# Hybrid layer on one core: norm statistics inside the mixer loop, the token table and all gate-up products ahead of the down products

## The reference, cut to what matters

```python
x = x + mixer(layernorm(x), ...)                    # state-space mixer, 8 groups of 1024 channels
x = x + ffn(layernorm(x), ...)                      # FFN, run 0
x = x + layernorm(x) @ (weight * block_mask).T      # block-sparse projection 512 -> 512
x = x + ffn(layernorm(x), ...)                      # FFN, run 1, same weights

def layernorm(x):  return (x - mean(x)) / sqrt(var(x) + 1e-5)

def ffn(x):
    g, u = split(x @ shared_w_gate_up.T, 2)         # 512 wide each
    shared = (silu(g) * u) @ shared_w_down.T
    probs = softmax(x @ gate_w.T)                   # 16 experts
    v, idx = top_k(probs, 2);  v = v / sum(v)
    # expert e: silu(x @ Wg_e.T) * (x @ Wu_e.T), 128 wide, then @ Wd_e.T
    moe = sum over the token's two experts of v * expert(x)
    return moe + shared
```

## Time and profile before

| what | value |
| --- | --- |
| median of 3 runs | 2115.55 us (2114.65 to 2116.76) |
| the profiled execution's own time | 2115.74 us |
| its span | 2114.0 us |
| granted TensorE clock, mean | 0.982 of full speed |
| busy share of the span | PE 94%, weight loads 78%, DVE 67%, ACT 55%, POOL 50% |
| mixer loop ends, all engines meet | 1666.1 us |
| first gate-up product, run 0 and run 1 | 1686.47 and 1920.41 us |

### The profile page before, as it was taken

One profiled execution on the slowest core, in us unless ns is written; L12 is line 12 of the kernel. 1 busy time (PEld: TensorE's weight loads), 2 busy tenths in 40 slices (PEclk: granted clock), 3 DMA queues, 4 the chain that ended last, 5 costly groups with the idle time before them and its releaser, 6 DMA issues.

```text
span 2114.0 us, 39207 instructions
## 1 busy us (share of the span) xinstructions
PE 1984.8 (94%) x11776; PEld 1643.1 (78%) x11776; DVE 1422.0 (67%) x2710; ACT 1172.9 (55%) x2553; POOL 1067.3 (50%) x955
## 2 busy tenths in 40 slices
PE   3899999999999999999999999999999889988998
PEld 2688878788878888888878888878888678766776
DVE  6697589749875976697579748974986551286214
ACT  2596368537843874496469537853884225321441
POOL 1288149705951793189239814970695125320423
PEclk8899999999999999999999999999999999999999
DMA  2453035114512341343135204521450349813895
GB/s 84 133 155 87 25 116 163 58 45 123 160 50 71 109 138 41 87 133 102 36 96 160 81 26 119 168 63 37 122 156 25 108 150 399 314 51 115 297 386 164
DMA packets 143908, 261.75 MB, mean 124 GB/s; under 512 B 19536, under 2 KB 35920, under 8 KB 143696
## 3 DMA queue, kind: packets, MB, share of 16 engines
q1 hardware_dynamic: 134848, 231.35, 34.6%
q0 software_dynamic: 7520, 24.65, 3.6%
q10 hardware_dynamic: 1328, 3.15, 0.4%
HBM read 233.38 MB, written 25.69 MB: 123 GB/s over the span
## 4 chain that ended last, share of the span: by engine, by line
PE 31%; issue 28%; DVE 23%; POOL 14%; ACT 2%; DVEq 1%; POOLq 0%; DMA 0%; ACTq 0%; SPq 0%
PE bank L1492 19%; DVE Y L1203 7%; POOL Y L711 7%; PE bank L1775 5%; DVE Y L1212 3%; PE bank L1787 3%; DVE mem L1171 3%; DVE mem L1191 3%; DVE Y L1228 2%; POOL wl L694 2%; POOL Y L661 1%; POOL spare L687 1%; POOL cv L687 1%; PE bank L1762 1%; POOL mem L673 1%
## 5 line engine op out<-in xcount | busy, mean ns | idle before, releaser
L1492 PE MATMUL bank<-xh,wh 128*128 128x512 f32 x1288 | 524.3, 407 | 16.5 <-POOL wl L694 12.9
L1492 PE MATMUL bank<-xh,wl 128*128 128x512 f32 x1288 | 505.5, 392 | 0.0
L1492 PE MATMUL bank<-xl,wh 128*128 128x512 f32 x1288 | 503.0, 391 | 0.0
L694 POOL TENSOR_TENSOR wl<-raw,wh 128x512 fp32r<-128x512 f32 x144 | 184.0, 1283 | 487.2 <-ACT wh L846 487.2
L1203 DVE SCALAR_TENSOR_TENSOR Y<-bank,cpar,Y 128x511 f32<-128x511 f32 (+2 forms) x384 | 287.0, 747 | 22.8 <-ACT Y L891 13.8
L1492 PEld LDWEIGHTS bank<-xh,wh 128*128 128x128 f32 x1288 | 243.4, 189 | 65.0 <-issue 18.0
L1492 PEld LDWEIGHTS bank<-xh,wl 128*128 128x128 f32 x1288 | 242.6, 188 | 54.4
L1492 PEld LDWEIGHTS bank<-xl,wh 128*128 128x128 f32 x1288 | 243.9, 189 | 46.0 <-issue 0.5
L1492 PE MATMUL bank<-wh,ah 128*128 128x512 f32 x576 | 229.4, 398 | 17.8 <-DVE al L1419 17.2
L1492 PE MATMUL bank<-wl,ah 128*128 128x512 f32 x576 | 227.0, 394 | 0.0
L1492 PE MATMUL bank<-wh,al 128*128 128x512 f32 x576 | 226.9, 394 | 0.0
(11 more groups left out here) (214 smaller groups left out, 3880.0 us busy)
## 6 DMA issues: line engine op xcount, KB each, us to landing
mem<-c_rows SPq DMA_DIRECT2D x128, 256.0 KB, 3.8
mem<-wffn_d SPq DMA_DIRECT2D x62, 512.0 KB, 8.2
E<-e_rows SPq DMA_DIRECT2D x256, 96.0 KB, 3.4
raw<-wconv_d SPq DMA_DIRECT2D x80, 256.0 KB, 2.8
cv<-c_rows SPq DMA_DIRECT2D x64, 256.0 KB, 3.9
spare<-c_rows SPq DMA_DIRECT2D x64, 256.0 KB, 4.2
raw<-wgate_d SPq DMA_DIRECT2D x64, 256.0 KB, 2.7
raw<-wout_d SPq DMA_DIRECT2D x64, 256.0 KB, 2.6
```

Of the source, the lines that this page charges most:

```text
L694: inc(pool.tensor_tensor(wl[:, W_SLOT[p], :], raw[:, R_SLOT[p], :], wh[:, W_SLOT[p], :], ALU.subtract), w_lo)
L1492: got = mm(out, l, r, start=first and n == 0, stop=last and n == 2)
```

## The change

Four things move. (1) In the mixer loop DVE takes the statistics of tile t - 1 behind the sum of tile t, in every group (only those of the last group are used), and the means of tiles 0 to 3 behind the sum of tile 6. ACT computes their square root and splits two weight pieces of the first shared block before the engines meet, for which SP loads four pieces before they meet. SP then asks for the mask ahead of the sparse weight. (2) `FFN_ORDER` has all four gate-up pairs ahead of all down products, in all four shared blocks; the hidden values of j = 2, 3 get places of their own in free rows of `wh` and `wl` (`hidden_rows`). (3) DVE computes the token table from the slots by a bit mask in place of five wide instructions, and between the parts of `hidden`; PE's `tokens` stands ahead of the down products. `own` moves behind the token list. (4) In the second blocks combine and sums are put in another order on DVE, and all six weight pieces for the third shared block are split inside norm 2.

```diff
@@ mixer loop, vector engine
                     t = k - NORM_AT
                     if 0 <= t < TT:
+                        if t:
+                            now(dve, res_ok, i, t)
+                        if t == CH + 2:
+                            now(dve, x_st, i, CH)
                         now(dve, big_mm, i, NCONV + NGATE + t + 1)
                         inc(STT(X[:, t, :], bank[big_bank(NCONV + NGATE + t)][:, :], rs8[:, t:t + 1], X[:, t, :],
                                 ALU.mult, ALU.add), res_ok)
+                        if t:
+                            inc(nc.vector.bn_stats(bst[:, t - 1, :], X[:, t - 1, :]), x_st)
+                        if t == CH + 2:
+                            for s in range(CH):
+                                inc(nc.vector.bn_aggr(mv[:, s, :], bst[:, s, :]), x_mv)
@@ vector engine, behind the loop
+            inverse1(0)
             phase_end(dve, PH_MIXER)
-            layer_norm(1)
+            xn1(0)
+            xn1(1)
+            stats1(TT - 1)
+            means1(1)
+            xn1(2)
+            lo1(0)
...
@@ scalar engine
-            phase_end(act, PH_MIXER)
+            deviations(1, 0)
...
+            for p in range(2):
+                w_part(0, p)
+            phase_end(act, PH_MIXER)
             layer_norm(1)
-            for p in range(6):
+            for p in range(2, 6):
                 w_part(0, p)
@@ order of the shared blocks, places of the hidden values
-        FFN_ORDER = [("gu", 0, 0), ("gu", 1, 0), ("gu", 0, 1), ("dn", None, 0), ("gu", 1, 1), ("dn", None, 1)]
+        FFN_ORDER = [("gu", 0, 0), ("gu", 1, 0), ("gu", 0, 1), ("gu", 1, 1), ("dn", None, 0), ("dn", None, 1)]
+        def hidden_rows(i, j, low):
+            if j < 2:
+                return (al if low else ah)[:, j, :, :]
+            s = (10, 0)[j - 2] if i % 2 else 7 + j
+            return (wl if low else wh)[:, s, :].rearrange("p (a b) -> p a b", a=4)
@@ vector engine, first shared block
-                hidden(first, 0)
-                hidden(first, 1)
+                hidden_gate(first, 0)
+                hidden_up(first, 0)
                 places()
-                for t in range(CH):
-                    add_down(first, t)
+                hidden_lo(first, 0)
+                hidden_gate(first, 1)
+                hidden_up(first, 1)
+                tiles_of_slots()
+                hidden_lo(first, 1)
+                rows_of_slots()
                 hidden(first, 2)
-                tokens_of_slots()
+                toks_out()
+                owners()
                 hidden(first, 3)
-                toks_out()
-                for t in range(CH, TT):
+                for t in range(TT):
                     add_down(first, t)
@@ vector engine, second shared block
+                hidden(second, 2)
                 combine(2)
-                hidden(second, 2)
                 combine(3)
-                for t in range(CH):
-                    dve.wait_ge(cmb, 2 * TT * run + 2 * (t + 1))
-                    add_down(second, t)
+                hidden(second, 3)
                 combine(4)
-                combine(5)
...
+                for t in range(CH):
+                    combined_down(t)
+                    if t == 1:
+                        combine(5)
+                    if run == 0:
                         stats2(t)
...
-                hidden(second, 3)
                 combine(6)
@@ tensor engine, first shared block
-                    if n == 4:
+                    if n == 3:
                         tokens()
```

More of the change, by code:

```diff
@@ L562, in _ @@
                 first, second = 2 * run, 2 * run + 1
+                for p in range(NRAW):
+                    shared_in(first, p)
                 if run == 0:
                     sp.wait_ge(phase, 4 * PH_MIXER)
+                    sp.dma_start(mski, mask_d.rearrange("k p n -> p k n")).then_inc(spm_in, 16)
                     sp.dma_start(wsp, wsp_d.rearrange("k p n -> p k n")).then_inc(sp_in, 16)
[L566 to L568 removed]
                 for p in range(NRAW, 6):
@@ L776, in step, with deviations @@
                 return steps[0]
-            def layer_norm(n):
-                def deviations(half):
-                    act.wait_ge(ln_mv, TT * n + CH * (half + 1))
-                    ts = slice(half * CH, (half + 1) * CH)
-                    nc.scalar.activation(sd8[:, ts], mv[:, ts, 1], ACT.Sqrt, bias=eps_c[:, 0:1]).then_inc(ln_sd, 1)
-                deviations(0)
-                if n < 2:
-                    deviations(1)
+            def deviations(n, half):
+                if n == 1 and half == 0:
+                    now(act, x_mv, GROUPS - 1, CH)
+                else:
+                    act.wait_ge(ln_mv, TT * n + CH * (half + 1))
+                ts = slice(half * CH, (half + 1) * CH)
+                nc.scalar.activation(sd8[:, ts], mv[:, ts, 1], ACT.Sqrt, bias=eps_c[:, 0:1]).then_inc(ln_sd, 1)
+            def layer_norm(n):
+                if n != 1:
+                    deviations(n, 0)
+                if n < 1:
+                    deviations(n, 1)
                 for t in range(TT):
+                    if n == 1 and t == 1:
+                        deviations(n, 1)
                     if n >= 2 and t == CH:
-                        deviations(1)
+                        deviations(n, 1)
                         if n == 2:
-                            for p in range(2, 6):
+                            for p in range(6):
                                 w_part(2, p)
@@ L1030, in _ @@
                 for j in range(4):
-                    if j == 3 and run == 0:
-                        for p in range(2):
-                            w_part(2, p)
                     hidden(second, j)
@@ L1449, in _, with combined_down @@
                     t_hidden(tau)
+                def combined_down(t):
+                    dve.wait_ge(cmb, 2 * TT * run + 2 * (t + 1))
+                    add_down(second, t)
                 hidden(second, 0)
@@ L1722, in down @@
                         for a in range(2):
-                            last = three(bank[ring[t % len(ring)]][:, :], ah[:, a, t % 4, :], al[:, a, t % 4, :],
+                            j = 2 * b + a
+                            last = three(bank[ring[t % len(ring)]][:, :], hidden_rows(i, j, 0)[:, t % 4, :],
+                                         hidden_rows(i, j, 1)[:, t % 4, :],
                                          wh[:, 3 * a + 2, :], wl[:, 3 * a + 2, :], a == 0, a == 1, True)
```

83 lines of the change are left out of this document (51 added, 32 removed).

## The result

The changed kernel takes 2088.24 us in the median (2087.14 to 2090.15), the kernel before 2115.1 us on the same chip: a ratio of 0.9873, 95% interval 0.9855 to 0.989. That is 26.9 us; forecast were 25.3 (2090.3 us). The profiled execution has a span of 2086.2 us, 27.8 less than before.

The account below looks back on a forecast made before the run. PE was taken to bound the kernel, busy 94% of the span, with its long waits ended by DVE and slowing its clock. Gains of 3.5 + 15.5 + 1.0 + 5.3 = 25.3 us gave 2090.3 us, range 2086 to 2100.

Parts of the forecast that it names:

- Loop, statistics: Mixer loop: the added statistics and means fit into DVE's waits and cost 0.
- Norm 1: Between mixer loop and first gate-up product: first normalised rows come earlier, net gain 3.5 us (1.9 to 4.2).
- the collision: Norm 1: POOL's split of two weight pieces slows DVE's second and third normalised rows, 0.7 us (0 to 2.3).
- First blocks: First shared blocks of both runs: PE's wait for the token table goes, net gain 15.5 us (9.6 to 16.0).
- DVE's list: First shared block: DVE's summed steps give the table at 1707.4, the token list at 1711.3, own at 1712.9.
- the wait at down tile 3: First shared blocks: a new PE wait of 1.0 us for a bank, queued behind DVE's fourth body.
- Tiles' input: Start of expert tiles: weights and gathers land with 1 us to spare; loss 0.25 us a run (0 to 3.2).
- The second rival: Expert tiles' input is late, 3.2 us lost a run, 2096 to 2097 us; chance 15%.
- Second blocks: Second shared blocks: shorter DVE waits, net gain 1.0 us in run 0 (0.5 to 2.8), 5.3 in run 1 (4.7 to 5.7).
- the slow clock of the projection: Behind run 0's second block: first 12 projection matmuls go from 2.98 to about 4.8 us, 1.8 us given back.
- The sum: Whole kernel: gains of 3.5 + 15.5 + 1.0 + 5.3 = 25.3 us, giving 2090.3 us.
- the 0.5 set aside for the tiles: Expert tiles of both runs: allowance of 0.25 us a run for late input, taken off the first blocks' gain.

Follow-up runs that it names:

- experiment 1: Kernel before, plus the loop's statistics and means written into tiles nothing reads, norm 1 still making its own: 2115.23 us against 2115.24, ratio 1.0001.
- experiment 10: Changed kernel with ACT's split of the first shared block's weight pieces 0 and 1 back behind norm 1: ratio 0.9863 [2086.1 us].
- experiment 8: Changed kernel with the owners' masks ahead of the tokens' cast on DVE, in its idle 1.25 us: ratio 0.9856 [2084.6 us].
- experiments 4 and 5: 4: changed kernel with PE's and DVE's old orders in second blocks, ratio 0.9871; 5: kernel before with new places for hidden values 2 and 3, 0.9954.
- experiment 3: Changed kernel with PE's order, DVE's order and the five wide table instructions as before in the first blocks of both runs: 2103.93 us, ratio 0.9945.
- experiment 7: Changed kernel with 20 unread matmuls on PE in its 5.57 us wait ahead of the second run's projection: ratio 0.9869 [2087.4 us].

## Why the prediction was right, point by point

**Loop, statistics: right.** 0 forecast, 0 measured (experiment 1).

**Norm 1: right.** 3.5 forecast, 3.3 measured. Within it the collision was taken at 0.7 us and cost PE 0.5 to 0.7: 16.94 us without it (experiment 10), against 17.4 at the least and 17.7 in the mean of the nine. Only parts of rows were hit, as forecast: 0.10 and 0.35 us. The Trainium skill, GPSIMD Engine Reference, section Specifications, says that GpSimd's shared SBUF interfaces contend with VectorE's instructions in a 2-port mode or with two SBUF inputs. The trace agrees that rows beside POOL are held up, but not with the full 0.97 us for each of two rows, which would have made the net gain 2.3 us.

**First blocks: right.** 15.5 forecast, 15.8 in the profiles, 15.7 by undoing them. DVE's list came out within half a microsecond, the wait at down tile 3 as 0.87 for 1.0. What was not seen is the 1.25 us of idle time ahead of the token list, though the forecast had both its sides: DVE's third body to 1710.1 and the list at 1711.3. Moving `own` there gives 2.3 us (experiment 8).

**Tiles' input: on time.** Rows on the SP queue and on POOL, and the DMA view of 1705 to 1712 us (KB each, us from issue to landing):

```profile
1711.47 0.41 SPq L551 DMA_DIRECT2D mem<-wffn_d  x1
```

```profile
1711.38 1.24 POOL L734 DMA_INDIRECT cv<-xn_dram,toks  x1 [27.29 <-DVE own L1420]
```

```profile
mem<-wffn_d SPq DMA_DIRECT2D x1, 512.0 KB, 3.4
cv<-xn_dram,toks POOLq DMA_INDIRECT x1, 4.4
```

Both were issued as the forecast had them, 2.2 us earlier on this trace's clock, and PE started on the tiles at 1720.78 with no wait. The second rival is out. There was more to spare than the forecast's 1 us: it took the medians of all loads and gathers (8.2 and 6.2 us), but the first load landed 3.4 us behind its issue and the first gather 4.4, some 5 us ahead of PE. Its bound of 3.2 us a run does not follow from its figures either, which give 2.6 (1725.7 less 1723.1).

**Second blocks: right in size, wrong in what pays.** Forecast +1.0 and +5.3, measured +0.7 and +5.7. The step that fails is its sum over "the change": it read rightly that DVE waits for a copy that waits for down products, and then priced order and places as one. The wait hangs on the places. With the old orders they give 4.7 us in run 0 (47.28 to 42.63) and 4.6 in run 1, and the orders take 4.0 back in the one and add 1.0 in the other (experiments 4 and 5). The greater part of what the order costs in run 0, the slow clock of the projection, was in the forecast: 1.8 us, measured 2.4. The 1.6 us in the block itself were not.

**The sum: right, in part by chance.** The terms in the profiles are 3.3 + 15.8 + 0.7 + 5.7 = 25.5 us against 25.3 (25.8 without the 0.5 set aside for the tiles). The rest of the profiles' 27.8 is 3.5 in the tiles less 1.2 in the loop. The loop's part is chance, and of the tiles' some 2 us may be the change's (experiment 3). The interval of the ratio (23.3 to 30.7 us of gain) is too wide to tell 25.5 from 27.5.

## What to carry to other kernels

When a change gives a buffer of its own to what used to share one and also reorders the work around it, price the two apart: here, with the old order, the buffer alone took the wait away, and the order that came with it cost 4 us in one of the two second blocks. In the first blocks it was the other way round: the buffers alone gave nearly nothing, and the order on top of them 14.5 us. A list that is emptied on one engine becomes idle time on the other, and where that is on TensorE, look whether the clock falls: behind idle times of 4.7 to 5.6 us the next twelve matmuls lost 1.3 to 2.5 us here, behind 0.7 to 2.2 us nothing. Look for an engine's short idle time just ahead of a result that it hands on, and put there what nobody waits for.

## What the runs showed of the hardware

**Results later than PE's own rows.** On the two other chips each of the eight kernels had at least one second block in which ACT and DVE got PE's results 2 to 6 us late. In the block shown below PE's rows follow each other every 0.227 us all the same, at a granted clock of 1.00; the ends of such rows are modelled. Timeline of ACT in run 1, changed kernel and then the kernel of experiment 7, which has the same order there:

```profile
2061.68 0.60 ACT L994 ACTIVATE gt<-bank 128x512 f32<-128x512 f32 x1 [1.30 <-PE bank L1556]
...
2067.12 0.60 ACT L994 ACTIVATE gt<-bank 128x512 f32<-128x512 f32 x1 [1.29 <-PE bank L1556]
```

```profile
2058.22 0.60 ACT L994 ACTIVATE gt<-bank 128x512 f32<-128x512 f32 x1 [1.29 <-PE bank L1556]
...
2068.11 0.60 ACT L994 ACTIVATE gt<-bank 128x512 f32<-128x512 f32 x1 [4.28 <-remote]
```

From the third to the fourth gate it is 5.44 us in the first and 9.89 in the second, for the same 24 matmuls. With the new order on PE the interval is 5.44 us or 8.5 to 11.3, with the old one 10.9 or 12.9 to 13.0 (and once 7.41 from the second gate to the third). It happens in blocks where results are gathered from DRAM all the time (DMA share 0.6 to 0.7), but also there not always, and never in the four profiles of the first chip, nor in those before and after. The kernel before is 5 to 6 us slower on those chips, which would fit one such block; no profile of it was taken there, and the cause stays open.

**The clock's price varies.** After the same wait of 5.57 us the same twelve matmuls took 5.46 us in two kernels and 4.31 in a third, and after 4.71 or 4.72 us 4.45 to 4.47 in three, against 2.99 at full clock: 1.3 to 2.5 us, and not in step with the idle time.
